# A three-slot Perceiver pipeline on one core: the block diagonals of head attention placed by SyncE, the first attention weights transposed on VectorE, the output bias added on GpSimd

## The chip, the cores and the metric

The kernel runs on one core of one Trainium2 chip. The metric is the device time of one execution in microseconds (us); the kernel before took 1451.5 us (median of three runs, 1449.05 to 1451.91).

The core has engines with instruction queues of their own: PE (TensorE) multiplies matrices and also transposes through an identity matrix, DVE (VectorE) and ACT (ScalarE) work element by element and read PE's results from PSUM, POOL (GpSimd) works on SBUF only, and SP (SyncE) only issues DMA transfers. Each engine runs its queue strictly in order. A semaphore wait at the head of a queue holds everything behind it.

## The reference, cut to what matters

There are 128 batch entries of 32 rows by 512 numbers. Each is normalized and goes through three blocks, each added to its input:

```python
x = x + xattn(layernorm(x), ctx)      # causal self attention, attention over 257 context rows, relu layer, norms
x = x + attn(layernorm(x))            # 16 heads of 32 columns, causal softmax times a decay, projection
x = x + ffn(layernorm(x))             # silu(x1) * x2, layer norm, second product, bias b3; experts for some rows

# the part of attn that the change touches
q, k, v = split(x @ W_attn)           # each cut into 16 heads
att = softmax(mask(q @ k.T / sqrt(32)))
att = att * decay
y = att @ v                           # per entry and head
# the part of xattn that it touches
p = softmax(mask(Q @ K.T) / sqrt(512))   # 32 x 32 per entry
a = p @ V + inputs
# the last step of the shared ffn
out = x2 + (z @ sw3.T + sb3)
```

Rows named by an index go a second time through one of eight experts; this is done at the end, and for the last tile inside the pipeline.

## The kernel before

Four entries of 32 rows stand together in one tile of 128 rows, so there are 32 tiles (0 to 31). A tile passes through all steps in four rounds. In each round four tiles are in work: the one just entered (lag 0), and those entered one, two and three rounds before (lags 1, 2, 3). Buffers exist three times (`rows1[s]`, `rows2[s]`, `rows3[s]`, `ps_a[s]`, `ps_t[s]` and others, with s the tile's number modulo 3; the third slot's SBUF buffers are parts of `last_slot`, which is the name that rows show for them).

The order on each engine is written out by hand. `FIRST` holds it for rounds 0 to 3, `ORDER` for rounds 4 to 29, `LAST` from round 30 on; `LOADS` holds it for SP in all rounds. An entry is a pair of a lag and a step's name, and `run_pipeline` issues the step for tile (round - lag). The same step name stands in the tables of several engines, each with its own part.

The steps around the change:

- `project_k`: PE computes the keys transposed, `high_t` and `low_t` (L1739, L1751), into `ps_a`. They must then stand in `kbd`, a block diagonal (for each entry and each group of four heads a 128 x 128 block in which each head's 32 keys fill their own 32 partitions), because `head_scores` on PE (L1814) handles four heads in one product. ACT writes the quarters of heads 0 and 1 (L850), DVE those of heads 2 and 3 (L1309).
- `head_scores`, `head_total`, `head_weights` on DVE: mask, maximum, subtraction, sum, reciprocal, product; then four 32-partition transposes (L1349) write the weights into `pbd`, a block diagonal over the four entries, for `head_mix` on PE (L1826). GpSimd multiplies by the decay (L653).
- `self_scores` on DVE scales, masks and takes the maximum; ACT exponentiates (L821); `turn_p` on PE transposes the 128 x 128 weights (L1770), ACT copies them to SBUF (L826), and `self_mix` on PE multiplies (L1775).
- `project_out` on DVE (L1355) makes x2 in `rows3`; `store_x2` on SP (L496) writes it to memory.
- `ffn_out` on DVE: one instruction for the product and b3 (L1389), one that adds x2 (L1391). `store` on SP (L500) writes the result.
- `xn_moments` and `turn_xn`: mean and variance of the tile just entered (L1178 to L1180), the inverse deviation on GpSimd (L636), the normalized rows on DVE (L1184), and their transposes on PE (L1703).

SP's order before, in a round: the next x, the context in transposed form (`load_ctx_t`, 2 MB, waits for the previous tile's `context_scores`), `store_x2` of the tile at lag 3, `store` of the same, then the context in plain form (`load_ctx_n`, 2 MB) and its last row (`ctx_last`).

## Time and profile before

| | |
|---|---|
| timed runs | 1451.91, 1449.05, 1451.5 us |
| profiled execution | span 1452.8 us; the page gives no time of its own beside the span, which lies 1.3 us above the median of the runs |
| busy | PE 1365.6 us (94%), weight loads 851.7, DVE 1128.1 (78%), ACT 601.9 (41%), POOL 526.1 (36%) |
| chain that ended last | PE 70%, DVE 19%, POOL 4%, ACT 4%, issue 3%, DMA 0% |
| DMA | 201.41 MB, 139 GB/s on the mean, busy three to four tenths |
| TensorE clock | nine tenths or more in 38 of the 40 slices, 8 tenths in the 2nd and the 38th |

A span is the time from the first to the last instruction. "PEclk" in a row of stretches is the clock that TensorE was granted, 1.00 for 2.4 GHz and 0.50 for 1.2 GHz. In a row of the time line the first number is the start, the second the duration, and what stands in brackets is the idle time before it and what ended it; nothing in brackets means that the engine was kept busy or that no releaser was found.

### The profile page before, as it was taken

The page shows a single profiled execution, that of the slowest core. Times are in us where ns is not written, and L with a number is a line of the kernel's source. Part 1 is how long each engine was busy: PE and PEld are TensorE (multiplying, and loading weights), DVE is VectorE, ACT ScalarE, POOL GpSimd, SP SyncE. Part 2 cuts the span into 40 slices and gives each one's busy share as a digit, 9 for nine tenths or more (in the row PEclk, how much of TensorE's full clock was granted, in tenths as well). Part 3 has the DMA queues.
Part 4 walks back from the last instruction along what each step waited for, and adds up shares of the span by engine and source line. Part 5 has one row for each costly group of instructions (what it writes and reads, how often), then busy time and mean ns, then how long its engine had stood idle before and what let it go on. Part 6 is the DMA issues. An engine that isn't in the chain of part 4 may idle for free.

```text
span 1452.8 us, 33270 instructions
## 1 busy us (share of the span) xinstructions
PE 1365.6 (94%) x13860; PEld 851.7 (59%) x13861; DVE 1128.1 (78%) x2335; ACT 601.9 (41%) x1147; POOL 526.1 (36%) x545
## 2 busy tenths in 40 slices
PE   7679999999999999999999999999999999998888
PEld 3355566666656666665665656666665666655443
DVE  6787777777787877778778877777778877777776
ACT  2544444443444444343434444444444444443222
POOL 0133333433444333443443333343443433343222
PEclk9899999999999999999999999999999999999899
DMA  9732444433333444433333344443333344434440
GB/s 349 259 131 74 146 146 146 144 123 105 133 112 115 146 146 146 146 137 101 122 130 105 139 146 146 146 142 114 111 138 105 123 146 146 147 134 161 149 161 30
DMA packets 38662, 201.41 MB, mean 139 GB/s; under 512 B 5096, under 2 KB 5992, under 8 KB 28400
## 3 DMA queue, kind: packets, MB, share of 16 engines
q1 hardware_dynamic: 37648, 198.93, 38.3%
q8 instruction: 109, 1.79, 0.5%
q10 hardware_dynamic: 864, 0.36, 0.1%
q14 instruction: 41, 0.34, 0.1%
HBM read 182.24 MB, written 17.04 MB: 137 GB/s over the span
## 4 chain that ended last, share of the span: by engine, by line
PE 70%; DVE 19%; POOL 4%; ACT 4%; issue 3%; DMA 0%; DVEq 0%; POOLq 0%; ACTq 0%; SPq 0%
PE ps_a L1716 11%; PE ps_a L1739 8%; PE ps_t L1739 7%; PE ps_t L1703 6%; PE ps_a L1725 6%; PE ps_a L1751 4%; PE ps_a L1783 4%; POOL rstd L636 4%; PE ps_t L1716 3%; PE ps_v L1716 3%; DVE stats L1178 3%; DVE arena L1309 3%; PE ps_t L1826 2%; PE ps_t L1775 2%; PE ps_t L1751 2%
## 5 line engine op out<-in xcount | busy, mean ns | idle before, releaser
L645 POOL TENSOR_TENSOR act_l<-act_t,act_h 128x512 f16<-128x512 f32 (+1 forms) x176 | 199.5, 1134 | 351.4 <-ACT act_t L789 199.4
L636 POOL TENSOR_TENSOR rstd<-var,mhalf 128x1 f32<-128x1 f32 x224 | 181.8, 812 | 333.7 <-DVE var L1180 328.9
L781 ACT ACTIVATE act_h<-ps_t,scale 128x512 f16<-128x512 f32 (+1 forms) x110 | 70.8, 644 | 206.2 <-PE ps_t L1703 206.2
L645 POOL TENSOR_TENSOR last_slot<-last_slot 128x512 f16<-128x512 f32 x80 | 90.0, 1125 | 156.7 <-ACT last_slot L789 90.8
L1739 PE MATMUL ps_a<-act_h,arena 128*128 128x128 f16 x1408 | 87.6, 221 | 17.3 <-ACT act_h L781 17.3
L1739 PEld LDWEIGHTS ps_a<-act_h,arena 128*128 128x128 f16 x1408 | 81.9, 99 | 28.3 <-ACT act_h L781 21.3
L789 ACT ACTIVATE act_t<-ps_t,scale 128x512 f32<-128x512 f32 (+1 forms) x110 | 70.3, 639 | 49.1 <-PE ps_t L1703 49.1
L1739 PE MATMUL ps_t<-act_h,arena 128*128 128x128 f16 x1408 | 87.0, 221 | 3.3 <-ACT act_h L781 3.3
L1716 PE MATMUL ps_a<-arena,act_h 128*128 128x512 f16 x352 | 83.6, 380 | 1.9 <-ACT act_h L781 1.9
L1309 DVE TENSOR_SCALAR arena<-ps_a,unscale 32x512 f32<-32x512 f32 x64 | 48.2, 753 | 47.0 <-PE ps_a L1751 45.8
L1739 PEld LDWEIGHTS ps_t<-act_h,arena 128*128 128x128 f16 x1408 | 81.4, 99 | 4.9 <-DVE arena L1037 2.4
L1178 DVE BATCH_NORM_STATS2 stats<-rows 128x6 f32<-128x512 f32 x110 | 76.5, 695 | 3.8
L781 ACT ACTIVATE last_slot<-ps_t,scale 128x512 f16<-128x512 f32 (+1 forms) x50 | 32.2, 644 | 89.4 <-PE ps_t L1703 89.4
L1191 DVE SCALAR_TENSOR_TENSOR rows<-rows,rstd,beta 128x512 f32<-128x512 f32 x66 | 50.2, 761 | 22.3 <-POOL rstd L636 22.2
L1716 PE MATMUL ps_a<-w_parts,act_h 128*128 128x512 f16 x264 | 64.2, 379 | 2.0 <-ACT act_h L781 2.0
L1703 PE MATMUL ps_t<-ident,rows 128*128 128x128 f32 x352 | 56.1, 283 | 9.1 <-DVE rows L1184 7.4
L1349 DVE STREAM_TRANSPOSE arena<-rows 32x512 f32<-32x512 f32 x88 | 61.8, 703 | 2.8
L1799 PE MATMUL ps_a<-arena,p_t 128*32 128x512 f32 x512 | 62.6, 607 | 0.0
L1716 PEld LDWEIGHTS ps_a<-arena,act_h 128*128 128x128 f16 x352 | 31.3, 98 | 50.6 <-ACT act_h L781 10.5
L1703 PEld LDWEIGHTS ps_t<-ident,rows 128*128 128x128 f32 x352 | 41.0, 143 | 29.0 <-DVE rows L1184 20.1
L1187 DVE SCALAR_TENSOR_TENSOR rows<-rows,mv,gamma 128x512 f32<-128x512 f32 x66 | 50.3, 762 | 0.0
L1783 PE MATMUL ps_a<-arena,q_t 128*32 128x257 f32 x704 | 44.2, 393 | 4.7 <-ACT q_t L830 4.7
(380 smaller groups left out, 3150.7 us busy)
## 6 DMA issues: line engine op xcount, KB each, us to landing
arena<-in_ctx_t SPq DMA_DIRECT2D x32, 2056.0 KB, 8.4
arena<-in_ctx_n SPq DMA_DIRECT2D x32, 2048.0 KB
ctx_last<-in_ctx_last SPq DMA_DIRECT2D x32, 256.0 KB
arena<-in_ew SPq DMA_DIRECT2D x8, 1024.0 KB, 6.3
x_in<-in_x SPq DMA_DIRECT2D x22, 256.0 KB, 7.3
x_scratch<-rows SPq DMA_DIRECT2D x22, 256.0 KB, 8.8
out<-rows SPq DMA_DIRECT2D x22, 256.0 KB, 2.1
arena<-in_ew SPq DMA_DIRECT2D x8, 512.0 KB, 7.2
```

The costliest lines, as they stand in the source:

```text
L636: nc.gpsimd.tensor_tensor(rstd[s][:], var[s][:], mhalf[:], ALU.pow).then_inc(rstd_ready[s], 1)
L645: nc.gpsimd.tensor_tensor(act_l[s][:, chunks], act_t[s][:, chunks], act_h[s][:, chunks], ALU.subtract).then_inc(act_l_ready[s], 1)
L781: nc.scalar.activation(act_h[s][:, 0:width // P].rearrange("p c r -> p (c r)"), bank[s][:, 0:width], ACT.Copy, scale=scale[:, k:k + 1]).th ...
L789: nc.scalar.activation(act_t[s][:, 0:width // P].rearrange("p c r -> p (c r)"), bank[s][:, 0:width], ACT.Copy, scale=scale[:, k:k + 1]).th ...
L1178: chain(nc.vector.bn_stats(stats[s][:], rows))
L1309: nc.vector.tensor_scalar(kbd[rows, :, :, h, :], ps_a[s][rows, :].rearrange("p (c g k) -> p c g k", c=C, g=G), unscale[rows, K_WATTN:K_WAT ...
L1703: mm = nc.tensor.transpose(out[s][:, c * P:(c + 1) * P], rows[s][:, lo + c * P:lo + (c + 1) * P], ident[:])
L1716: nc.tensor.matmul(bank[s][:], act_h[s][:, c, :], w[:, part, c, lo:lo + D], start=(c == 0 and part == 0), stop=False, skip_group_check=True)
L1725: mm = nc.tensor.matmul(bank[s][:], act_l[s][:, c, :], w[:, 0, c, lo:lo + D], start=False, stop=(c == chunks - 1), skip_group_check=True)
L1739: nc.tensor.matmul(bank[s][:, m * P:(m + 1) * P], w[:, part, c, lo + m * P:lo + (m + 1) * P], act_h[s][:, c, :], start=(m == 0 and c == 0 ...
L1751: mm = nc.tensor.matmul(bank[s][:, m * P:(m + 1) * P], w[:, 0, c, lo + m * P:lo + (m + 1) * P], act_l[s][:, c, :], start=False, stop=(c == ...
L1783: mm = nc.tensor.matmul(ps_a[s][T * g:T * (g + 1), 0:S], q_t[s][:, c, T * g:T * (g + 1)], ctx_t[:, c, g, :], start=(c == 0), stop=(c == C ...
```

## The change

- `project_k`: ACT writes all keys in one instruction, dense, into `rows3` of the slot (semaphore `k_out`). DVE's two instructions are gone. A new step `heads_k` on SP copies them by four SBUF to SBUF transfers of 64 KB (one for each 32 partitions) into `kbd`; PE's `head_scores` waits for all four. `kbd` is laid out anew, with the head outermost, so that a partition's 2 KB are contiguous at the destination; PE now reads 4 pieces of 32 numbers each.
- `head_weights`: DVE transposes once over 128 partitions into `rows3` (`heads_turned`), and a new step `heads_p` on SP copies to `pbd` by four transfers of 64 KB; `head_mix` waits for them.
- `turn_p` moves from PE and ACT to DVE, as one 128 x 128 instruction that transposes 32 x 32 blocks, together with the reciprocal that `self_mix` had.
- `ffn_out` is one DVE instruction. b3 is added ahead of it to x2 in `rows3` by the new step `x2_bias` on GpSimd, which waits until x2 is normalized and until `store_x2` has landed.
- The scale of the exponent goes into `unscale`, so that the negative maximum comes straight from the reduction: one small instruction less in `self_scores` and `context_scores`.
- Some waits of DVE for its own previous instruction move from behind it to the instruction that reads the result (`made_by`).

```diff
-LOADS = [(0, "load_x"), (0, "set_first"), (0, "set_rest"), (0, "load_ctx_t"),
+LOADS = [(0, "load_x"), (0, "set_first"), (0, "set_rest"), (0, "load_ctx_t"), (2, "heads_k"),
          (3, "store_x2"), (1, "e_first"), (1, "e_second"), (1, "e_rows"), (2, "e_fifth"), (3, "store"),
-         (0, "load_ctx_n"), (1, "e_third"), (1, "e_fourth"), (2, "e_sixth")]
+         (0, "load_ctx_n"), (2, "heads_p"), (1, "e_third"), (1, "e_fourth"), (2, "e_sixth")]
...
+                def heads_k(s, r, tile):
+                    sp.wait_ge(k_out, tile + 1)
...
+                    for h in range(HPC):
+                        mine = slice(HD * h, HD * (h + 1))
+                        sp.dma_start(kbd[mine, h, :, :, :].rearrange("p c g k -> p (c g k)"), rows3[s][mine, :]
+                                     ).then_inc(k_ready, 16)
+
+                def heads_p(s, r, tile):
+                    sp.wait_ge(heads_turned, tile + 1)
...
+                    for g in range(G):
+                        mine = slice(T * g, T * (g + 1))
+                        sp.dma_start(pbd[mine, g, :, :].rearrange("p h q -> p (h q)"), rows3[s][mine, :]
+                                     ).then_inc(pbd_ready, 16)
...
+                def x2_bias(s, r, tile):
+                    pool.wait_ge(rows_ready[s], 6 * r + 5)
+                    pool.wait_ge(x2_stored[s], 16 * r + 32)
...
+                    nc.gpsimd.tensor_tensor(rows3[s][:], rows3[s][:], b3[:], ALU.add).then_inc(x2_biased, 1)
...
                 def project_k(s, r, tile):
                     act.wait_ge(k_done[s], r + 1)
...
-                    for h in (0, 1):
-                        rows = slice(HD * h, HD * (h + 1))
-                        nc.scalar.activation(kbd[rows, :, :, h, :],
...
+                    nc.scalar.activation(rows3[s][:], ps_a[s][:], ACT.Copy, scale=unscale[:, K_WATTN:K_WATTN + 1]
+                                         ).then_inc(k_out, 1)
...
+                def turn_p(s, r, tile):
+                    chain = Chain("turn_p", s, r)
+                    dve.wait_ge(p_ready[s], 3 * r + 1)
+                    nc.vector.transpose(p_t[s][:, 0:P], p_n[s][:, 0:P]).then_inc(p_t_ready[s], 1)
+                    chain.last(nc.vector.reciprocal(inv[s][:, 0:1], total[s][:, 0:1]))
...
-                    for g in range(G):
-                        rows = slice(T * g, T * (g + 1))
-                        nc.vector.transpose(pbd[rows, :, g, :], by_head(rows1[s][rows, :])).then_inc(pbd_ready[s], 1)
+                    nc.vector.transpose(sc, by_head(rows1[s][:])).then_inc(heads_turned, 1)
...
                 def ffn_out(s, r, tile):
                     dve.wait_ge(rows_done[s], 6 * r + 6)
-                    chain = Chain("ffn_out", s, r)
-                    chain(nc.vector.scalar_tensor_tensor(rows2[s][:], ps_a[s][:], unscale[:, K_W3:K_W3 + 1], b3[:],
-                                                         ALU.mult, ALU.add))
-                    nc.vector.tensor_tensor(rows2[s][:], rows2[s][:], rows3[s][:], ALU.add).then_inc(out_ready[s], 1)
-                    chain.end()
+                    dve.wait_ge(x2_biased, tile + 1)
+                    nc.vector.scalar_tensor_tensor(rows2[s][:], ps_a[s][:], unscale[:, K_W3:K_W3 + 1], rows3[s][:],
+                                                   ALU.mult, ALU.add).then_inc(out_ready[s], 1)
...
-                pe.wait_ge(pbd_ready[s], 4 * r + 4)
+                pe.wait_ge(pbd_ready, 64 * (tile + 1))
```

The tables of DVE lose `project_k` and gain `turn_p` between `context_norm` (lag 1) and `self_mix` (lag 0); those of PE and ACT lose `turn_p`; those of POOL gain `x2_bias` (lag 3) ahead of `xn_moments` (lag 0).

Three places show what this does to the queues. First SP in a regular round, before. `arena` is the buffer that holds weights, context and the block diagonals.

```order
L482 DMA arena<-in_ctx_t 128x4112 [waits scored1]
L496 DMA x_scratch<-last_slot 128x512 [waits x2_ready2]
L500 DMA out<-last_slot 128x512 [waits out_ready2]
L489 DMA arena<-in_ctx_n 128x4096 [waits v_done1]
L492 DMA ctx_last<-in_ctx_last 128x1x512 [waits v_ready1]
L475 DMA x_in<-in_x 128x512 [waits x_used0]
L482 DMA arena<-in_ctx_t 128x4112 [waits scored2]
```

The same round of SP with the change (L510 is `heads_k`, L521 is `heads_p`):

```order
L482 DMA arena<-in_ctx_t 128x4112 [waits scored1]
L510 DMA arena<-rows 32x512 [waits scored2,k_out]
L510 DMA arena<-rows 32x512 x3
L496 DMA x_scratch<-last_slot 128x512 [waits x2_ready2]
L500 DMA out<-last_slot 128x512 [waits out_ready2]
L489 DMA arena<-in_ctx_n 128x4096 [waits v_done1]
L492 DMA ctx_last<-in_ctx_last 128x1x512 [waits v_ready1]
L521 DMA arena<-rows 32x512 [waits y_done2,heads_turned]
L521 DMA arena<-rows 32x512 x3
L475 DMA x_in<-in_x 128x512 [waits x_used0]
```

The store of x2 (L496), which stood right behind the context load, now stands behind a wait for the keys of the tile at lag 2 and four issues.

Second, DVE between `z_norm` of the tile at lag 3 and the normalized rows of the tile at lag 0, before:

```order
L1191 SCALAR_TENSOR_TENSOR last_slot<-last_slot,rstd,ln_b 128x256 [waits rstd_ready2,dve_step2]
L1309 TENSOR_SCALAR arena<-ps_a,unscale 32x16x32 [waits scored2,k_done0]
L1309 TENSOR_SCALAR arena<-ps_a,unscale 32x16x32
L1389 SCALAR_TENSOR_TENSOR last_slot<-ps_a,unscale,b 128x512 [waits rows_done2]
L1391 TENSOR_TENSOR last_slot<-last_slot 128x512 [waits dve_step2]
L1178 BN_STATS stats<-last_slot 128x6 [waits x_loaded2]
L1179 BN_AGGR mv<-stats 128x2 [waits dve_step2]
L1180 TENSOR_SCALAR var<-mv 128x1 [waits dve_step2]
L1246 RECIPROCAL inv<-total 128x1 [waits p_ready1]
L1184 TENSOR_SCALAR last_slot<-last_slot,mv,rstd 128x512 [waits rstd_ready2]
```

DVE there with the change:

```order
L1218 SCALAR_TENSOR_TENSOR last_slot<-last_slot,rstd,ln_b 128x256 [waits dve_step2,rstd_ready2]
L1399 SCALAR_TENSOR_TENSOR last_slot<-ps_a,unscale,last_slot 128x512 [waits x2_biased,rows_done2]
L1204 BN_STATS stats<-last_slot 128x6 [waits x_loaded2]
L1205 BN_AGGR mv<-stats 128x2 [waits dve_step2]
L1206 TENSOR_SCALAR var<-mv 128x1 [waits dve_step2]
L1273 RECIPROCAL inv<-total 128x1 [waits p_ready1]
L1210 TENSOR_SCALAR last_slot<-last_slot,mv,rstd 128x512 [waits rstd_ready2]
```

Three instructions are gone; the one that makes the output (L1399) now waits for GpSimd, and what the tile at lag 0 needs stands behind it.

Third, DVE between the self scores of the tile at lag 0 and its mix, before (L1268 to L1187 is `context_out` of the tile at lag 1, L1227 is `self_mix`):

```order
L1213 SCALAR_TENSOR_TENSOR last_slot<-ps_a,unscale,mask_self 128x128 [waits x2_stored2,scored2]
L1216 TENSOR_REDUCE top<-last_slot 128x1 [waits dve_step2]
L1217 TENSOR_SCALAR ntop<-top 128x1 [waits dve_step2]
L1268 SCALAR_TENSOR_TENSOR rows<-ps_a,row_out,rows 128x512 [waits rows_done1]
L1178 BN_STATS stats<-rows 128x6 [waits dve_step1]
L1179 BN_AGGR mv<-stats 128x2 [waits dve_step1]
L1180 TENSOR_SCALAR var<-mv 128x1 [waits dve_step1]
L1187 SCALAR_TENSOR_TENSOR rows<-rows,mv,gamma 128x512
L1191 SCALAR_TENSOR_TENSOR rows<-rows,rstd,beta 128x512 [waits rstd_ready1,dve_step1]
L1224 RECIPROCAL inv<-total 128x1 [waits p_ready2]
L1227 SCALAR_TENSOR_TENSOR last_slot<-ps_t,inv,last_slot 128x512 [waits out_stored2,rows_done2,dve_step2]
```

With the change (L1296 to L1213 is `context_out`, L1249 the new transpose, L1258 `self_mix`):

```order
L1240 SCALAR_TENSOR_TENSOR last_slot<-ps_a,unscale,mask_self 128x128 [waits x2_stored2,scored2]
L1243 TENSOR_REDUCE ntop<-last_slot 128x1 [waits dve_step2]
L1296 SCALAR_TENSOR_TENSOR rows<-ps_a,row_out,rows 128x512 [waits dve_step1,rows_done1]
L1204 BN_STATS stats<-rows 128x6 [waits dve_step1]
L1205 BN_AGGR mv<-stats 128x2 [waits dve_step1]
L1206 TENSOR_SCALAR var<-mv 128x1 [waits dve_step1]
L1213 SCALAR_TENSOR_TENSOR rows<-rows,mv,gamma 128x512
L1218 SCALAR_TENSOR_TENSOR rows<-rows,rstd,beta 128x512 [waits dve_step1,rstd_ready1]
L1249 STREAM_TRANSPOSE p_t<-p_n 128x128 [waits p_ready2]
L1250 RECIPROCAL inv<-total 128x1
L1258 SCALAR_TENSOR_TENSOR last_slot<-ps_t,inv,last_slot 128x512 [waits out_stored2,dve_step2,rows_done2]
```

Before, PE transposed these weights as soon as ACT had them; now the transpose stands behind five instructions for the tile at lag 1 and GpSimd's inverse deviation.

## Rows read from the trace of the kernel before

**Rows 1.** Busy times of a stretch: length, busy us of each engine, PEclk, DMA share, GB/s.
```profile
400.00:1200.00 800.00, 777.21 (x8357) 494.95 (x8355) 633.82 (x1322) 342.58 (x670) 315.96 (x315) 1.00 0.37 130
```

**Rows 2.** Time line of SP's issues, round 15 and the start of round 30.
```profile
634.72 0.33 SPq L482 DMA_DIRECT2D arena<-in_ctx_t  x1
635.09 0.43 SPq L496 DMA_DIRECT2D x_scratch<-rows  x1
644.82 0.34 SPq L500 DMA_DIRECT2D out<-rows  x1
646.20 0.34 SPq L489 DMA_DIRECT2D arena<-in_ctx_n  x1
...
1244.22 0.33 SPq L482 DMA_DIRECT2D arena<-in_ctx_t  x1
```

**Rows 3.** The chain that ended last, in order of time, in round 15.
```profile
640.82 0.91 PE ps_a L1751 x16
641.75 0.75 DVE arena L1309
...
643.32 0.76 DVE rows L1389
644.10 0.69 DVE rows L1391
...
647.07 0.66 PE ps_t L1703 x4
```

**Rows 4.** Time line of ACT, round 15.
```profile
642.03 1.37 ACT L850 ACTIVATE arena<-ps_a,unscale 32x512 f32<-32x512 f32 x2
...
644.32 0.69 ACT L856 ACTIVATE q_t<-ps_t,unscale 128x512 f32<-128x512 f32 x1 [0.52 <-PE ps_t L1751]
```

**Rows 5.** DMA issues: KB each, median us from issue to landing.
```profile
out<-rows SPq DMA_DIRECT2D x22, 256.0 KB, 2.1
```

**Rows 6.** Groups of instructions, 400 to 1200 us: busy, mean ns, idle before.
```profile
L653 POOL TENSOR_TENSOR rows<-rows,decay 128x512 f32<-128x512 f32 x13 | 16.6, 1280 | 12.4 <-ACT rows L866 12.4
```

**Rows 7.** Time line of PE, round 15.
```profile
645.95 1.06 PE L1814 MATMUL ps_a<-arena,q_t 128*32 128x128 f32 x32
...
659.16 0.27 PE L1770 MATMUL ps_a<-ident,p_n 128*128 128x128 f32 x1
...
660.38 1.13 PE L1775 MATMUL ps_t<-v_n,p_t 128*128 128x512 f32 x2
```

**Rows 8.** Time line of DVE, round 15.
```profile
654.13 2.90 DVE L1349 STREAM_TRANSPOSE arena<-rows 32x512 f32<-32x512 f32 x4
...
657.84 0.74 DVE L1268 SCALAR_TENSOR_TENSOR last_slot<-ps_a,row_out,last_slot 128x512 f32<-128x512 f32 x1
...
660.88 0.75 DVE L1191 SCALAR_TENSOR_TENSOR last_slot<-last_slot,rstd,beta 128x512 f32<-128x512 f32 x1 [0.51 <-POOL rstd L636]
```

**Rows 9.** Busy times of two stretches in round 2, columns as in rows 1.
```profile
101.00:104.00 3.00, 1.04 (x12) 0.72 (x9) 2.40 (x2) 1.11 (x2) 0.55 (x1) 0.93 0.67 170
104.00:107.00 3.00, 3.00 (x31) 3.00 (x30) 2.86 (x8) 0.73 (x3) 2.70 (x2) 0.50 0.99 422
```

**Rows 10.** The chain that ended last, round 2: one product's two halves.
```profile
103.72 3.48 PE ps_a L1739 x32
107.20 1.79 PE ps_t L1739 x32
```

**Rows 11.** Time line of SP's issues, round 32.
```profile
1331.95 0.47 SPq L518 DMA_DIRECT2D last_slot<-x_scratch  x1
...
1344.06 0.33 SPq L545 DMA_DIRECT2D ctx_last<-in_sel_g  x1
```

**Rows 12.** Time line of DVE, round 32.
```profile
1338.78 1.54 DVE L1309 TENSOR_SCALAR arena<-ps_a,unscale 32x512 f32<-32x512 f32 x2 [1.43 <-PE ps_a L1751]
...
1346.41 0.69 DVE L1404 BATCH_NORM_STATS2 stats<-last_slot 128x6 f32<-128x512 f32 x1 [1.02 <-DMA last_slot<-x_scratch]
...
1360.96 0.69 DVE L1480 TENSOR_TENSOR last_slot<-ps_a,arena 128x512 f32<-128x512 f32 x1
```

More of the change, by code:

```diff
@@ L146 @@
         (1, "e_gate_c"), (1, "e_bias0"), (2, "e_bias3"), (0, "self_scores"), (2, "e_z3"), (1, "e_z0"),
-        (1, "context_out"), (0, "self_mix")],
+        (1, "context_out"), (0, "turn_p"), (0, "self_mix")],
     "act": [(3, "head_mix_t"), (3, "head_mix"), (2, "turn_h2"), (2, "turn_h2_t"), (2, "e_zt0"), (2, "e_gate1"),
@@ L820, in self_scores @@
                     act.wait_ge(ntop_ready[s], 2 * r + 1)
-                    nc.scalar.activation(p_n[s][:, 0:P], rows3[s][:, 0:P], ACT.Exp, bias=ntop[s][:], scale=XSCALE,
+                    nc.scalar.activation(p_n[s][:, 0:P], rows3[s][:, 0:P], ACT.Exp, bias=ntop[s][:],
                                          accum_out=total[s][:, 0:1]).then_inc(p_ready[s], 1)
-                def turn_p(s, r, tile):
-                    act.wait_ge(p_turned[s], 2 * r + 1)
-                    nc.scalar.copy(p_t[s][:, 0:P], ps_a[s][:, 0:P]).then_inc(p_t_ready[s], 1)
                 def project_query(s, r, tile):
@@ L843, in project_k @@
                     act.wait_ge(k_done[s], r + 1)
-                    if tile == 0:
-                        act.wait_ge(consts_ready, 4)
-                    else:
-                        act.wait_ge(scored[(s - 1) % SLOTN], 3 * (r - (s == 0)) + 3)
-                    for h in (0, 1):
-                        rows = slice(HD * h, HD * (h + 1))
-                        nc.scalar.activation(kbd[rows, :, :, h, :],
-                                             ps_a[s][rows, :].rearrange("p (c g k) -> p c g k", c=C, g=G), ACT.Copy,
-                                             scale=unscale[rows, K_WATTN:K_WATTN + 1]).then_inc(k_ready[s], 1)
+                    nc.scalar.activation(rows3[s][:], ps_a[s][:], ACT.Copy, scale=unscale[:, K_WATTN:K_WATTN + 1]
+                                         ).then_inc(k_out, 1)
                 def project_q(s, r, tile):
@@ L1167, in __call__, with last @@
                     def __call__(self, ins):
+                        self.last(ins)
+                        dve.wait_ge(dve_step[self.s], steps_in_all * self.r + steps_before[self.unit] + self.count)
+                    def last(self, ins):
                         self.count += 1
@@ L1270, in context_out @@
                     moments(chain, s, rows3[s][:], 1e-3)
-                    chain(scaled(s, rows1[s][:], rows3[s][:], gamma[:]))
+                    chain.last(scaled(s, rows1[s][:], rows3[s][:], gamma[:]))
                     chain.end()
                 def context_norm(s, r, tile):
-                    offset(s, r, 3, rows1[s][:], beta[:]).then_inc(rows_ready[s], 1)
+                    offset(s, r, 3, rows1[s][:], beta[:], "context_out").then_inc(rows_ready[s], 1)
                 def hidden(s, r, tile):
@@ L1285, in hidden @@
                     moments(chain, s, rows3[s][:], 1e-3)
-                    chain(scaled(s, rows2[s][:], rows3[s][:], gamma[:]))
+                    chain.last(scaled(s, rows2[s][:], rows3[s][:], gamma[:]))
                     chain.end()
@@ L1369, in ffn_in @@
                     chain = Chain("ffn_in", s, r)
-                    chain(nc.vector.scalar_tensor_tensor(v_n[s][:, H:], rows2[s][:, 0:H], 0.5, rows2[s][:, H:],
+                    chain.last(nc.vector.scalar_tensor_tensor(v_n[s][:, H:], rows2[s][:, 0:H], 0.5, rows2[s][:, H:],
                                                          ALU.mult, ALU.mult))
@@ L1766, in self_scores @@
                     mm.then_inc(scored[s], 1)
-                def turn_p(s, r, tile):
-                    pe.wait_ge(p_ready[s], 3 * r + 1)
-                    nc.tensor.transpose(ps_a[s][:, 0:P], p_n[s][:, 0:P], ident[:]).then_inc(p_turned[s], 1)
                 def self_mix(s, r, tile):
@@ L1810, in head_scores @@
                     pe.wait_ge(q_ready[s], 4 * r + 4)
-                    pe.wait_ge(k_ready[s], 4 * r + 4)
+                    pe.wait_ge(k_ready, 64 * (tile + 1))
                     for c in range(C):
```

131 lines of the change are left out of this document (63 added, 68 removed), and 1 row of the table FIRST.

## The prediction

> **What bounds the kernel now.** I read the busy times by stretch first. In 800 us of regular rounds PE is busy 777.2 us, DVE 633.8, at the full clock throughout [rows 1]: PE is the bound, and all that it ever idles there is 22.8 us, 1.16 us in a round. A round is the distance between two context loads: from 634.72 (round 15) to 1244.22 (round 30) 609.5 us, so 40.63 us [rows 2]. Nothing that unloads DVE, ACT or PE's waits can give back more than that 1.16 us. Then I read the chain of waits in order of time, because PE's slack is thin in one place: after the keys of the tile at lag 2 (end 641.73) the chain leaves PE, runs through DVE (block diagonal, output, moments) and GpSimd, and comes back at 647.07 with the transposes of the tile just entered [rows 3]. PE has other work meanwhile, and that work ends just when DVE delivers. Whatever makes DVE later between 641.7 and 647.1 is paid one for one. Last I read SP's time line, since the change puts waits into that queue.
>
> **Part 1: the output waits for GpSimd, GpSimd for the store, the store for the keys.** Taken away on DVE are the two block diagonal writes (1.54 us) and the addition L1391 (0.69) [rows 3, 12]. In their place stands a wait. I follow it through round 15. PE ends the keys at 641.73. ACT starts on them at 642.03, behind its exponentials, and one full instruction takes 0.69 us [rows 4]: keys in SBUF at 642.72. SP issues four transfers. One issue behind another started 0.37 us apart (634.72 to 635.09), and the second took 0.43 itself [rows 2]; I take 0.45 each, 1.8 us. Only then comes the store of x2, which went out at 635.09 before: now at about 644.6. A 256 KB store into an idle queue lands 2.1 us after its issue [rows 5]: 646.7. GpSimd adds b3; the nearest row is its 128x512 product with the decay, 1.28 us [rows 6]: 648.0. DVE starts the output there and not at 643.32, that is 4.8 us later [rows 3]; since L1391 (0.78 from start to start) is gone, the moments of the new tile start 4.0 us later. GpSimd's inverse deviation and the normalization follow as before, so PE's transposes start at about 651.1. PE idles for the **4.0 us**. Bounds: issues at 0.37 and the landing at 2.0 make it 3.6; issues at 0.55 and 1.4 us more for a store that mixes with the 256 KB of the four transfers make it 5.8.
>
> What is queued behind this wait on DVE is all of the rest of the round, but its later instructions follow the same tile or PE itself, so they shift with PE and add nothing. In the same gap hides the latency of the block diagonal of the keys: its transfers land at about 646.5, PE's `head_scores` needs them at 645.95 [rows 7], and PE would idle until 651.1 anyway. If that cover were gone it would cost some 0.6 us.
>
> The Trainium skill (DMA: Bandwidth & Descriptors, Anatomy of one DMA) gives a fixed part of about 2.0 us and 436 GB/s on top, fitted for transfers issued by GpSimd: 2.6 us for this store, where the row has 2.1. With the page's price the sum would be 14 us higher; the row decides.
>
> **Part 2: the head weights.** DVE's four transposes (2.90 us, 0.73 each) become one, and four transfers follow [rows 8]. In the new time scale DVE ends that transpose about 7.8 us after PE's transposes start (654.13 less 647.07, plus 0.7), SP issues until 9.6, the last lands at about 11.7 by the 2.1 us of [rows 5]. PE needs the block at 12.1 after (659.16 less 647.07) [rows 7]. It fits with 0.4 us to spare, provided the plain context load, which SP issued at 646.20 [rows 2] and which will now go out about 3.5 us later behind the delayed store of the output, is through. Cost nothing; without that cover 1 to 3 us a round. PE reads its block in four pieces now; the trace has no such operand. Below: nothing gained; above: the 1.08 us product could double. I take nothing.
>
> **Part 3: the transpose of the self weights on DVE.** PE loses L1770, whose successor starts 0.20 us later; the product behind it ran until 660.38 [rows 7]. But DVE puts the transpose behind `context_out` and `context_norm` of the other tile. Freed from the block transposes, DVE can start L1268 at about 656.8, when PE has its product, instead of 657.84 [rows 8]. From there to the end of L1191 the trace has 3.79 us (657.84 to 661.63), with GpSimd's deviation inside: 660.6. The transpose: one of 512 columns takes 0.73, so one of 128 between 0.2 and 0.4; with 0.3: 660.9. PE would be ready for `self_mix` at 660.2; before it started at 660.38. So it starts **0.5 us** later than before, and the removed work is already in this number. Bounds 0.2 (a faster transpose) and 0.9 (the same chain with a later start).
>
> **Part 4: the clock of TensorE.** In round 2, PE was busy 1.04 us in the 3 us from 101 to 104, and in the next 3 us the granted clock was 0.50, the lower of its two levels, 1.2 GHz [rows 9]. The first half of a product of 64 small matmuls then took 3.48 us, the second half, at the full clock, 1.79 [rows 10]: 1.7 us lost. With the change PE has in every round a stretch like it: about 0.6 us idle ahead of `head_scores`, that product, and some 3.4 us idle behind it. I expect the clock to fall in most rounds, sometimes before the gap's end so that part of the low time costs nothing: **1.3 us** a round on the mean; bounds 0 and 2.3.
>
> The Trainium skill (TensorE: Matmul & The Clock Gate, HAM oscillation) tells that a kernel whose matmuls wait for a transfer in every iteration pays the half clock in every iteration. The trace agrees in the one place where it has such a gap; regular rounds of before have none.
>
> **Part 5: the ends.** In rounds 0 to 3 DVE is itself on the path and gains a little, the store chain costs once (round 3): +4 us together. The end costs more. In round 32 SP used to read x2 of the last routed tile back at 1331.95, behind ten expert issues, because nothing held it; it is awaited by DVE at 1346.41 [rows 11, 12]. Now all this stands behind the keys of tile 30, which PE has at 1338.78 [rows 12]: 0.75 us for ACT, 1.8 for the block, 0.45 for the store, 4.7 for the ten issues at the 0.47 of [rows 11]: read back at 1346.5, and by the same 14.4 us as before landed at 1360.9: 14.5 late. The expert biases were issued at 1344.06 [rows 11]; now they stand behind the head weights, which DVE had done some 0.9 us before it added the first bias at 1360.96 [rows 12], and will have at 1360.1 - 2.2 + 14.5 = 1372.4. With 1.8 for the block, 4.6 for their own eight issues and about 5.5 to land (an estimate, above the 2.1 of rows 5 because 2 MB stand in the queue): 1384.3, so 23.3 late in all. Round 33 adds the store chain (4.0) and the weights' transfers on an exposed chain (3.9 for 2.2): 5.7; the dropped addition gives 0.7 back. Together **+28 us**; bounds 12 (the read-back lands sooner, since only part of the 5 MB is ahead) and 38.
>
> **The sum.** 28 regular rounds (4 to 31) at 4.0 + 0.5 + 1.3 = 5.8 us: 162. With 4 and 28: 194. The profiled execution spans 1452.8 us, 1.3 above the median of the runs: 1452.8 + 194 - 1.3 = **1646 us**. Lowest terms: 3.6 + 0.2 + 0 for 28 rounds, 0, 12: 1570. Highest: 5.8 + 1.1 + 0.9 + 2.3 for 28 rounds, 10, 38: 1782.
>
> **Rivals.**
> A, the clock holds: everything else as above, 28 x 1.3 less: 1610. For it: gaps of about 1 us in regular rounds left the clock at 1.00 [rows 1]. Against: [rows 9]. 25%.
> B, the head weights' transfers queue behind the plain context load and its last row, which now starts later; PE waits again at `head_mix`, 2.5 us a round: 1646 + 70 = 1716. For it: the 0.4 us of spare time is thin. Against: GpSimd and DVE leave the queue 10 us from the load's issue. 12%.
> C, the other side: the bias is added in time and DVE's relief decides. It holds only if x2's store lands and GpSimd is done before DVE reaches the output, at 641.8 instead of 648.0; then PE loses L1770 (0.2 us a round) and some of its 1.16 us: about 1451.5 - 28 x 0.3 = 1443. For it: DVE does lose about 4.4 us of work a round. Against: the order of SP's queue leaves the store no way past the keys. 3%; no change at all 2%.
> The forecast itself: 58%.
>
> **Chances.** Slower by over 0.2% (about what a measurement of this kernel can tell from no change) 0.95, within 0.2% 0.02, faster 0.03. The range for 8 in 10, across the forecast and most of A and B: 1590 to 1708.
>
> **What would show it.** Right: SP's store of x2 issued 10 us after the context load, not 0.4; DVE idle some 7 us before the output instruction with GpSimd's addition as its releaser; PE idle about 3.4 us before L1703's counterpart with DVE as releaser; a second idle of 0.5 us before `self_mix`; a round of 46 to 47 us; PEclk below 1.00 in regular rounds; DVE's first expert moments 15 us late against PE's keys in round 32. Wrong: a round under 43 us, or a store that is issued before the keys' transfers.

## The result, and the profile after

The changed kernel takes **1713.69 us** (median of four runs, 1712.18 to 1714.39) where the kernel before, on the same chip, takes 1451.7 (1449.05 to 1452.14): ratio 1.181, interval 1.180 to 1.183. The forecast was 1646 us with a range of 1590 to 1708. The direction and the mechanism came as predicted; the time lies 68 us above the forecast and 6 us outside the range. The question is therefore which terms were too small.

Busy times of the stretch from 400 to 1200 us of the changed kernel, columns as in [rows 1]:

```profile
400.00:1200.00 800.00, 691.59 (x7092) 428.18 (x7092) 464.40 (x1002) 278.44 (x539) 286.68 (x283) 0.94 0.36 124
```

PE is idle 108.4 us of these 800 where it was idle 22.8, and the granted clock is 0.94 instead of 1.00. DVE works 169 us less in the same time: some 74 of that are relief (4.4 us a round, an estimate from these busy times and the lengths of a round), the rest comes from fewer rounds in the 800 us. More waiting and a slower clock, with no engine busier than before: no engine has become the bound, a chain has. A round, from context load to context load, has 47.8 us (732.91 to 780.78) instead of 40.63.

SP's issues in the round that begins at 732.91 (start, duration), to be laid beside [rows 2]:

```profile
732.91 0.33 SPq L482 DMA_DIRECT2D arena<-in_ctx_t  x1
740.95 2.41 SPq L510 DMA_DIRECT2D arena<-rows  x4
743.40 0.58 SPq L496 DMA_DIRECT2D x_scratch<-rows  x1
747.94 0.35 SPq L500 DMA_DIRECT2D out<-rows  x1
...
759.94 2.44 SPq L521 DMA_DIRECT2D arena<-rows  x4
```

The store of x2 goes out 10.5 us behind the context load and no longer 0.37. The four issues ahead of it take 2.41 us, 0.61 each from start to start. The same chain on ACT, POOL and DVE, from the keys' way into SBUF to the normalized rows of the new tile:

```profile
740.22 0.70 ACT L869 ACTIVATE rows<-ps_a,unscale 128x512 f32<-128x512 f32 x1
...
745.80 1.26 POOL L685 TENSOR_TENSOR rows<-rows,b 128x512 f32<-128x512 f32 x1 [5.10 <-DMA x_scratch<-rows]
...
747.16 0.75 DVE L1399 SCALAR_TENSOR_TENSOR rows<-ps_a,unscale,rows 128x512 f32<-128x512 f32 x1 [8.79 <-POOL rows L685]
...
749.59 0.55 DVE L1210 TENSOR_SCALAR rows<-x_in,mv,rstd 128x512 f32<-128x512 f32 x1 [0.59 <-POOL rstd L658]
```

Each releaser is the one of the prediction: DVE's output waits for POOL, POOL for the store. PE in the same round:

```profile
738.84 1.06 PE L1759 MATMUL ps_a<-act_l,arena 128*128 128x128 f16 x16
...
744.90 1.08 PE L1818 MATMUL ps_a<-arena,q_t 128*32 128x128 f32 x32 [0.57 <-DMA arena<-rows]
750.19 1.12 PE L1711 MATMUL ps_t<-ident,rows 128*128 128x128 f32 x4 [4.21 <-DVE rows L1210]
751.10 3.43 PE L1724 MATMUL ps_v<-arena,act_h 128*128 128x512 f16 x8
...
764.33 1.08 PE L1830 MATMUL ps_t<-arena,v_n 128*32 128x128 f32 x32
765.86 1.12 PE L1779 MATMUL ps_t<-v_n,p_t 128*128 128x512 f32 x2 [0.45 <-DVE p_t L1249]
```

The first row is that of the keys, done at 739.90 (738.84 and 1.06). Then four things are to be seen: `head_scores` waits a little for the keys' transfers, the transposes wait 4.21 us for DVE, the product behind them takes 3.43 us (1.89 elsewhere), and `self_mix` waits 0.45 us for DVE's transpose. `head_mix` (L1830) waits for nothing here. The clock of the gap and of the product, in stretches of 1 us (length, busy times, then PEclk, third from the end):

```profile
745.00:746.00 1.00, 0.98 (x32) 0.71 (x31) 0.00 (x0) 0.00 (x0) 0.20 (x1) 1.00 0.19 72
746.00:747.00 1.00, 0.00 (x0) 0.00 (x0) 0.00 (x0) 0.00 (x0) 1.00 (x1) 1.00 0.00 0
747.00:748.00 1.00, 0.00 (x0) 0.00 (x0) 0.84 (x2) 0.00 (x0) 0.06 (x1) 0.69 0.00 0
...
753.00:754.00 1.00, 1.00 (x4) 0.30 (x2) 0.32 (x2) 1.00 (x3) 0.84 (x1) 0.50 0.96 410
754.00:755.00 1.00, 1.00 (x14) 0.79 (x13) 0.95 (x3) 0.73 (x2) 0.81 (x1) 0.90 1.09 459
```

The clock falls to its lower level, 1.2 GHz, while PE idles, and stays there through the product. From the transposes (750.19) to the next projection (754.36) the trace has 4.17 us. Before, at the full clock, the same stretch took 2.22, from 647.07 [rows 3] to this row:

```profile
649.29 1.95 PE L1739 MATMUL ps_a<-act_h,arena 128*128 128x128 f16 x32
```

So 1.95 us are lost. The Trainium skill (TensorE: Matmul & The Clock Gate, HAM oscillation) describes a kernel whose products wait for a transfer in every iteration and start every iteration at the half clock. The trace agrees, with a wait for DVE in place of the transfer: the granted clock is 0.94 from 400 to 1200 us, where it was 1.00.

### The profile page after: what moved, and what is told of

It reads as the page before. It is cut to its first block and busy times, and to the rows that moved or that the text cites. A ratio compares the mean times of both kernels' runs of the same rounds, so it can differ in the third digit from the quotient of the medians.

```text
span 1710.4 us, 33273 instructions
## 1 busy us (share of the span) xinstructions
PE 1427.2 (83%) x13828; PEld 866.9 (51%) x13829; DVE 989.3 (58%) x2112; ACT 575.1 (34%) x1083; POOL 564.7 (33%) x577
## 5 line engine op out<-in xcount | busy, mean ns | idle before, releaser
L1711 PE MATMUL ps_t<-ident,rows 128*128 128x128 f32 x352 | 64.0, 312 | 98.8 <-DVE rows L1210 95.0
L1399 DVE SCALAR_TENSOR_TENSOR rows<-ps_a,unscale,rows 128x512 f32<-128x512 f32 x22 | 16.5, 751 | 192.7 <-POOL rows L685 192.7
L1711 PEld LDWEIGHTS ps_t<-ident,rows 128*128 128x128 f32 x352 | 45.5, 156 | 119.5 <-DVE rows L1210 106.8
L1711 PE MATMUL ps_t<-ident,last_slot 128*128 128x128 f32 x220 | 37.4, 292 | 41.5 <-DVE last_slot L1210 41.1
L1724 PE MATMUL ps_v<-arena,act_h 128*128 128x512 f16 x176 | 70.0, 571 | 0.0
L685 POOL TENSOR_TENSOR rows<-rows,b 128x512 f32<-128x512 f32 x22 | 27.8, 1262 | 115.3 <-DMA x_scratch<-rows 107.0
L1399 DVE SCALAR_TENSOR_TENSOR last_slot<-ps_a,unscale,last_slot 128x512 f32<-128x512 f32 x10 | 7.5, 751 | 91.5 <-POOL last_slot L685 91.5
```

The source lines that it names most:

```text
L685: nc.gpsimd.tensor_tensor(rows3[s][:], rows3[s][:], b3[:], ALU.add).then_inc(x2_biased, 1)
L1399: nc.vector.scalar_tensor_tensor(rows2[s][:], ps_a[s][:], unscale[:, K_W3:K_W3 + 1], rows3[s][:], ALU.mult, ALU.add).then_inc(out_ready[s], 1)
L1711: mm = nc.tensor.transpose(out[s][:, c * P:(c + 1) * P], rows[s][:, lo + c * P:lo + (c + 1) * P], ident[:])
L1724: nc.tensor.matmul(bank[s][:], act_h[s][:, c, :], w[:, part, c, lo:lo + D], start=(c == 0 and part == 0), stop=False, skip_group_check=True)
```

## The experiments

The theory (T) is the chain of the prediction, with the sizes of the trace after: keys, four issues, store, addition, output, transposes, and the clock that falls in the gap. All runs are whole kernels; each edit is made to the changed kernel, except in `before_bias`.

**Moving the store ahead of the keys** (store_first):

```diff
-LOADS = [(0, "load_x"), (0, "set_first"), (0, "set_rest"), (0, "load_ctx_t"), (2, "heads_k"),
-         (3, "store_x2"), (1, "e_first"), (1, "e_second"), (1, "e_rows"), (2, "e_fifth"), (3, "store"),
+LOADS = [(0, "load_x"), (0, "set_first"), (0, "set_rest"), (0, "load_ctx_t"), (3, "store_x2"),
+         (2, "heads_k"), (1, "e_first"), (1, "e_second"), (1, "e_rows"), (2, "e_fifth"), (3, "store"),
```

> SP issues the store of x2 before it waits for the keys, all else as in the changed kernel. Theory T (the store stands behind the keys' wait and four issues, GpSimd's addition behind its landing, DVE's output and all of lag 0 behind that, and the clock falls in the gap): the wait of DVE L1399 for GpSimd goes, the clock stays at 1.00, and what is left of a round's loss is PE's wait for the keys' own transfers (0.9 us) and the late self_mix (0.4): a round of 41.9 us, 1520 us in all (1500 to 1545, the end still about 30 late). Rival U (the loss lies in the eight transfers themselves, or in PE's reading of the new block layouts): above 1650 us.

Measured: 1551.03 us (1549.35 to 1553.94), ratio 1.070 (1.068 to 1.071). The 163 us that go show that the place of one issue in SP's queue carries most of the loss, and rule U out. The 31 us above my figure are a miss, outside T's range. The mean round has 42.7 us, not 41.9, which makes 20 of them; the rest is mostly the opening (context load 4 at 199.50, before at 188.32). SP's, POOL's and DVE's rows of the round that begins at 757.26:

```profile
757.64 0.43 SPq L496 DMA_DIRECT2D x_scratch<-last_slot  x1
...
766.73 1.29 POOL L685 TENSOR_TENSOR last_slot<-last_slot,b 128x512 f32<-128x512 f32 x1 [1.68 <-DMA x_scratch<-last_slot]
...
768.12 0.75 DVE L1399 SCALAR_TENSOR_TENSOR last_slot<-ps_a,unscale,last_slot 128x512 f32<-128x512 f32 x1 [5.40 <-POOL last_slot L685]
```

The store was issued at once and landed 9 us later, beside 2 MB of context that was issued 0.38 us ahead of it. DVE still waits 5.4 us, PE 0.78 (and 0.60 for the keys); the usual round has 42.5 us, some 45 to 47. The transfer of 2.1 us in [rows 5] was one into an idle queue. That the store of x2 is slow in this place stood in the trace of before (KB, median us from issue to landing), where nobody waited for it, and T could have priced it:

```profile
x_scratch<-rows SPq DMA_DIRECT2D x22, 256.0 KB, 8.8
```

The Trainium skill (DMA: Bandwidth & Descriptors, Issuing engines are not separate DMA queues) says that DMAs run on the same 16 engines and interleave, whoever issues them. The 8.8 us of the median store here fit that, beside a load with a median of 8.6. Whether the store is served between the load's pieces or behind them, no run shows.

**Undoing the addition on GpSimd** (bias_undone; `x2_bias` also leaves GpSimd's tables):

```diff
-                    dve.wait_ge(x2_biased, tile + 1)
-                    nc.vector.scalar_tensor_tensor(rows2[s][:], ps_a[s][:], unscale[:, K_W3:K_W3 + 1], rows3[s][:],
-                                                   ALU.mult, ALU.add).then_inc(out_ready[s], 1)
+                    chain = Chain("ffn_out", s, r)
+                    chain(nc.vector.scalar_tensor_tensor(rows2[s][:], ps_a[s][:], unscale[:, K_W3:K_W3 + 1], b3[:],
+                                                         ALU.mult, ALU.add))
+                    nc.vector.tensor_tensor(rows2[s][:], rows2[s][:], rows3[s][:], ALU.add).then_inc(out_ready[s], 1)
+                    chain.end()
...
```

> DVE makes the output in two instructions again with b3 and x2, GpSimd's addition is gone, SP's order stays as changed, with the store of x2 behind the keys. Theory T: cutting the chain at this link does the same as moving the store: 1525 us, within 10 us of it; the 0.69 us more on DVE hides. Rival V (it is the late store, and behind it the late store of the output and the late plain context load, that hold the round, not the addition): above 1600 us.

Measured: 1531.14 us (1528.32 to 1533.95), round 41.65. V is out: SP's late store hurts by the addition that waits for it, not by itself. The round is 1.02 us above before, and PE's rows name it: 0.59 for the keys' transfers (the 0.6 that the prediction gave them without their cover), 0.45 for DVE's transpose. Of the 74 us that this trace is longer than that of before, 12 lie ahead of round 4, 31 in rounds 4 to 30 and 31 behind the last context load.

**Store between the wait and the issues** (store_between): `heads_k` waits for the keys, then issues the store of x2, then its four transfers.

> The store of x2 still stands behind SP's wait for the keys, but ahead of the four issues. Theory T with the size read from the trace of the changed kernel (four issues of 0.61 us each, where I had taken 0.45): the store goes 2.45 us earlier and 26 rounds get 2.4 us shorter, 1645 us (1630 to 1665). With issues of 0.45 us it would be 1663. Rival W (the size error came from the store's landing beside the four transfers, which now start together with it): the gain is under 1 us a round, above 1688 us.

Measured: 1603.55 us (1594.96 to 1608.15), 41 us better than T's figure and outside its range. The store is no slower beside the transfers (DVE's output starts 3.6 us after its issue, 3.8 in the changed kernel), so W is out. Rounds come in two lengths, 43.3 and 45.0 us: 47.8 less 2.45 is 45.35, and less the 1.95 of the clock 43.4. The transposes of two rounds and the product behind them show it:

```profile
749.82 1.11 PE L1717 MATMUL ps_t<-ident,rows 128*128 128x128 f32 x4 [1.19 <-DVE rows L1216]
750.73 3.08 PE L1730 MATMUL ps_v<-arena,last_slot 128*128 128x512 f16 x8
...
794.69 0.66 PE L1717 MATMUL ps_t<-ident,last_slot 128*128 128x128 f32 x4 [1.12 <-DVE last_slot L1216]
795.18 1.89 PE L1730 MATMUL ps_v<-arena,act_h 128*128 128x512 f16 x8
```

The wait for DVE is down from 4.21 us to 1.2 (the keys' transfers, issued behind the store, now hold `head_scores` longer), and the clock falls in some rounds only. T forgot that the gain of a shorter wait can come twice.

**Keeping the clock up in the gap** (clock_kept):

```diff
                     mm.then_inc(scored[s], 1)
+                    if 3 <= tile <= 27:
+                        for n in range(16):
+                            nc.tensor.matmul(ps_e[:], w3[:, 0, 0, 0:P], w3[:, 0, 0, :], start=True, stop=True,
+                                             skip_group_check=True)
```

> As the changed kernel, but PE does 16 extra half-precision products of 512 columns into a bank that nobody reads, behind head_scores of tiles 3 to 27 (some 3.5 us at the full clock), in the gap where it waits for the transposes of lag 0. The chain of the store is untouched. Theory T: the clock stays at 1.00, the self projection takes its full speed again, 1.95 us a round in 25 rounds: 1665 us (1655 to 1685). Rival X (the clock cost nothing, what looks slow was waiting for something else): 1705 to 1720 us.

Measured: 1667.86 us (1667.37 to 1670.13), 45.8 us less than the changed kernel by work that nobody needs. Its round has 45.93 us, 1.9 less than 47.83, and PE's rows show the gap filled and the product at its full speed:

```profile
727.36 3.63 PE L1825 MATMUL ps_e<-w_parts 128*128 128x512 f16 x16
731.63 0.66 PE L1711 MATMUL ps_t<-ident,rows 128*128 128x128 f32 x4 [0.64 <-DVE rows L1210]
732.13 1.89 PE L1724 MATMUL ps_v<-arena,act_h 128*128 128x512 f16 x8
```

The clock term is shown, with its size: 1.9 us a round.

**The store ahead of the context load** (bias_early_store): `(3, "store_x2")` stands before `(0, "load_ctx_t")`.

> SP issues the store of x2 ahead of the context load and not behind it (in the run with the store merely ahead of the keys it landed 9 us after its issue, beside 2 MB of context, and GpSimd's addition still came 5.4 us late for DVE). Theory T (only the landing of the store makes the addition late): the store lands in some 2.3 us, long before the keys are done, DVE waits for GpSimd no more, and the round is that of the run with the addition undone, 41.65 us: 1530 us (1520 to 1540). Rival Y (the addition itself holds GpSimd's queue in a bad place, or slows DVE): above 1540 us.

Measured: 1526.42 us (1525.73 to 1529.8), usual round 41.65. The median store lands 2.1 us after its issue, and PE waits for nothing of the chain any more. So the addition on GpSimd is free once its store is early; the 187 us between this run and the changed kernel are the price of its place, not of its work. Y is out.

**The transpose of the self weights earlier** (turn_p_early): in DVE's tables for rounds 0 to 29 `(0, "turn_p")` stands before `(1, "context_norm")`.

> As the changed kernel, with DVE's transpose of the self weights ahead of context_norm of the other tile, where DVE waits 0.44 us for GpSimd anyway, in rounds 0 to 29. Theory T: PE's 0.45 us ahead of self_mix goes (1.76 us in rounds 1 to 3), and every round gets shorter by that: 1713.7 less 26 x 0.43 less 4 is 1698 us (1690 to 1704). Rival: the wait only moves to the next thing that DVE makes (x2 or the norm for the other tile): 1709 to 1718 us.

Measured: 1707.2 us (1701.98 to 1708.23), ratio 1.175 against 1.181: 6.5 us, not 16, between the ranges of T and of the rival. PE's wait of 0.45 is gone, but the round only fell from 47.83 to 47.76. The rest went into the clock. Its stretches at the start and the end of the low time, in the round from 919.32 (PE idle from 932.4, transposes at 936.63):

```profile
933.00:934.00 1.00, 0.00 (x0) 0.00 (x0) 0.39 (x1) 0.00 (x0) 0.51 (x1) 1.00 0.00 0
934.00:935.00 1.00, 0.00 (x0) 0.00 (x0) 0.96 (x3) 0.00 (x0) 0.00 (x0) 0.79 0.00 0
...
940.00:941.00 1.00, 1.00 (x4) 0.35 (x3) 0.86 (x4) 1.00 (x3) 0.65 (x2) 0.50 0.94 393
941.00:942.00 1.00, 1.00 (x16) 1.00 (x15) 0.53 (x2) 0.18 (x1) 0.91 (x1) 0.79 0.77 311
```

The transposes start earlier in the low time here than in the changed kernel: the clock is back some 4.8 us after their start, there some 4.0. The product takes 3.62 us instead of 3.43 and the projection behind it 2.17 instead of 1.95, together 0.4 us. In all of six rounds between 746 and 986 us that product has 3.62. What a wait saved, the low clock took. That both are one effect is read from the rows; no run varied this alone.

**The head weights written by DVE** (weights_direct): four transposes into `pbd`, no transfers.

> As the changed kernel, but DVE writes the head weights into their block diagonal itself, by four transposes of 32 partitions, and the four transfers are gone. Theory T: in regular rounds the transfers cost PE nothing, but they relieve DVE of 2.2 us on the way to the transpose of the self weights, so undoing them makes self_mix about 1.0 us later: +26 us; in rounds 2 and 3, where head_mix stands early and PE waited 2.6 and 1.9 us for the transfers, it gives 4.5 back: 1735 us (1722 to 1745). Rival Z (the transfers cost the round something through the queues): at or under 1713 us.

Measured: 1727.02 us (1725.84 to 1727.86). Undoing this part alone makes the kernel slower by 13 us. PE's wait before `self_mix` grew from 0.45 to 1.32 us, as reckoned, since DVE has 2.2 us more ahead of its transpose. The 13 us are a balance: rounds 4 to 29 take 31 us more, the parts outside them less. In round 2 the load of the next context came 4.2 us sooner (44.14 against 48.35 us for the round), in round 3 1.4, and from the last context load to the end it has 198.0 us against 209.1: there the transfers do cost. At the end DVE no longer waits for the expert biases, which stood behind them in SP's queue (12.9 us in the changed kernel).

**The expert loads ahead of the keys** (experts_first), on top of store_first:

```diff
-         (2, "heads_k"), (1, "e_first"), (1, "e_second"), (1, "e_rows"), (2, "e_fifth"), (3, "store"),
-         (0, "load_ctx_n"), (2, "heads_p"), (1, "e_third"), (1, "e_fourth"), (2, "e_sixth")]
+         (1, "e_first"), (1, "e_second"), (1, "e_rows"), (2, "heads_k"), (2, "e_fifth"), (3, "store"),
+         (0, "load_ctx_n"), (1, "e_third"), (2, "heads_p"), (1, "e_fourth"), (2, "e_sixth")]
```

> As the run with the store of x2 ahead of the keys (1551 us), and the expert loads and the read-back of x2 also ahead of the keys, the expert biases ahead of the head weights. It concerns round 32 alone. Theory T (the end's loss, 30.4 us there after the last context load, is mostly these loads standing behind keys and head weights): it falls by 20 to 25 us, 1529 us (1524 to 1536). Rival (the end loses by the transfers of keys and weights in an exposed chain, and the loads hardly matter): above 1543 us.

Measured: 1531.01 us (1527.68 to 1537.4), 20 less than store_first. From the last context load to the end it has 176.1 us, store_first 197.1, before 166.7. DVE's wait for the read-back of x2 fell from 17.19 us to 1.88:

```profile
1424.28 0.70 DVE L1412 BATCH_NORM_STATS2 stats<-last_slot 128x6 f32<-128x512 f32 x1 [1.88 <-DMA last_slot<-x_scratch]
```

**The keys written by ACT and DVE** (keys_direct): `project_k` on both engines as before, no transfers, SP's order else as changed.

> As the changed kernel, but ACT and DVE write the keys' block diagonal and the four transfers are gone, SP's order otherwise the same: the store of x2 follows the context load at once. Theory T: it lands 9 us after its issue, as in the run with the store ahead of the keys, the addition is as late as there, and PE loses about as much per round (42.3 to 42.6 us); the end is shorter, since only the last expert loads stand behind the head weights: 1535 us (1520 to 1550). Rival (without the transfers of the keys the addition is in time): under 1505 us.

Measured: 1536.24 us (1528.68 to 1543.19), in T's range, with a mean round of 43.0 us (a little above T's) and most of them 41.5 to 43.1. The store follows the context load at once and is as late as in store_first. Without the early store, taking the keys off SP does not save the addition.

**What is left of the change without transfers** (all_direct): keys and weights written directly, store ahead of the context load, `turn_p` early.

> The changed kernel without its eight transfers (ACT and DVE write the keys' block diagonal, DVE that of the weights), with the store of x2 ahead of the context load and DVE's transpose of the self weights ahead of context_norm. What stays of the change: the addition of b3 on GpSimd, the self weights' transpose on DVE, the negated maximum, the own waits at their consumers. Theory T: PE is the bound; of its 1.11 us of waits in a round of before (0.78 for ACT behind the transposes of x1, 0.33 for DVE behind those of x2) none is touched, so DVE's relief gives nothing, and PE saves the transpose alone, 0.20 us a round: 40.43 us a round, 1446 us, ratio 0.996 (0.993 to 0.999). Rival: DVE's relief of some 1.5 us a round also shortens PE's waits, below 1440 us; or an addition on GpSimd costs DVE, above 1452 us.

Measured: 1449.97 us (1444.78 to 1450.83, 11 runs) against 1449.63, ratio 0.9995 (0.9986 to 1.0004): no change. The round has 40.54 us, 0.10 less than before and not 0.20. DVE works 11.8 us less in the stretch of 800 (622.01, before 633.82), and it gains nothing to see. Neither T's range nor the rival's holds the result. 26 rounds at 0.10 would give 2.6 us, and the median lacks them. Ten of the eleven executions have a mean granted clock of 0.987 or 0.988; the eleventh has 0.992 and took 1444.78. Of the sixteen executions of before, fourteen have 0.991 or 0.992. So the clock outside the regular rounds may take back what they give; no run varied that alone.

**The kernel before with the early addition alone** (before_bias): the added step, the one-instruction output and `(3, "store_x2")` ahead of `(0, "load_ctx_t")`.

> The kernel before with one part of the change: b3 is added on GpSimd and DVE makes the output in one instruction; SP issues the store of x2 ahead of the context load so that the addition is in time. Theory T: DVE loses 0.69 us a round that nobody waited for, PE's two waits stay, 1450 us, ratio 1.000 (0.998 to 1.002). Rival: DVE was on the path between the keys and the new tile's transposes, and PE's round gets shorter by some of it: ratio under 0.996.

Measured: 1445.7 us (1444.94 to 1447.84), ratio **0.9966** (0.9953 to 0.9978). It is faster than before by 3.9 us, little but clear of the interval, and neither side's figure was quite right. The round is 40.50 us, 0.13 less. The place is the one the prediction called thin: `head_scores` to the transposes of the new tile, 1.12 us apart in [rows 3, 7] (645.95, 647.07) and now 0.99, the time that the product itself needs:

```profile
806.77 1.06 PE L1819 MATMUL ps_a<-arena,last_slot 128*32 128x128 f32 x32
807.76 0.66 PE L1708 MATMUL ps_t<-ident,rows 128*128 128x128 f32 x4
```

Before, DVE delivered 0.13 us late, too little for the trace to show as a wait; the 0.69 of the dropped addition removed that and no more. This is read from the rows: no run moved the store without dropping the addition. 26 rounds at 0.13 are 3.4 us of the 3.9 between the medians. The two traces also differ behind the last context load (163.1 against 166.7 us), but they are single executions, and from 1350 to 1360 us the granted clock is 0.85 here and 0.52 in that of before.

## Why the time was missed: the prediction's steps, one by one

The mechanism of every large term held, and four sizes failed: the chain of the store (4.0 us a round forecast, 4.9 measured, most of it the issues at 0.45 us each that take 0.61), the clock (1.3 forecast, 1.95 measured), the opening (4 forecast, 18.3 measured, with the exposed head weights of rounds 2 and 3 not priced at all) and the end.

**The output waits for GpSimd, GpSimd for the store, the store for the keys** (Part 1): right in every link, too small in size. Predicted from the end of the keys to DVE's output 6.27 us, measured 7.26 (739.90 to 747.16). Of the 0.99 us, 0.65 are the issues: a 64 KB transfer from 32 partitions takes SP 0.61 us, and I had taken 0.45 from a load and a store of another shape. 0.3 are the store's landing (2.4 us to GpSimd's start, 2.1 assumed). ACT took the keys 0.3 us after their end, as forecast. PE's transposes start 10.29 us after the end of the keys, before 5.34: 4.9 us later, not 4.0. The 4.0 also holds a slip: 648.0 less 643.32 is 4.7 and not 4.8, so the sum should have had 3.9. The upper bound of 5.8 held it. store_between, bias_undone and bias_early_store show the chain link by link.

**The head weights** (Part 2): right for regular rounds, where PE waits for nothing at `head_mix`, and where the transfers even help DVE (weights_direct). Wrong for rounds 2 and 3, which I had not worked out: their table has `head_mix` earlier on PE, ahead of `self_scores`, so that the transfers are exposed (2.58 and 1.87 us). The table stood in the code. The operand in pieces, for which I took nothing, costs nothing to see: `head_scores` takes 1.08 us (1.06 before) and `head_mix` 1.08 as before.

**The transpose on DVE** (Part 3): 0.5 predicted, 0.45 waited; from the transposes of the new tile to `self_mix` it is 0.4 more than before, the clock's 1.95 taken off. Right.

**The clock** (Part 4): the mechanism right, and the 1.3 us were 0.65 too little: I averaged over rounds in which the clock would stay; at a gap of 4.2 us it fell in all that I looked at. 1.95 measured by duration, 1.9 by clock_kept. Rival A (the clock holds) was worth 25% and is dead. Round 2 was also not "the one place" of before with a gap and a low clock: it had 0.67 from 60 to 70 us and 0.52 from 1350 to 1360.

**The ends** (Part 5): the opening was to cost 4 us and cost 18.3 (context load 4 at 206.64 instead of 188.32). 4.9 of it are round 2: the exposed weights' transfers, and 1.76 us before `self_mix`, whose transpose stands in that table behind a whole `project_out`. 13.8 are round 3, where the chain of the store meets a table in which PE has nothing else to do:

```profile
169.00 1.11 PE L1711 MATMUL ps_t<-ident,rows 128*128 128x128 f32 x4 [8.26 <-DVE rows L1210]
...
185.28 1.08 PE L1830 MATMUL ps_t<-arena,v_n 128*32 128x128 f32 x32 [1.87 <-DMA arena<-rows]
192.78 1.12 PE L1779 MATMUL ps_t<-v_n,p_t 128*128 128x512 f32 x2 [1.76 <-DVE p_t L1249]
```

"The store chain costs once (round 3)" was the right thought with the wrong price. At the end, the read-back and the biases are awaited where I said, each a little later still:

```profile
1586.45 0.69 DVE L1412 BATCH_NORM_STATS2 stats<-last_slot 128x6 f32<-128x512 f32 x1 [12.67 <-DMA last_slot<-x_scratch]
1611.33 0.69 DVE L1488 TENSOR_TENSOR last_slot<-ps_a,arena 128x512 f32<-128x512 f32 x1 [12.88 <-DMA arena<-in_ew]
```

From the last context load they come at 85.2 and 110.1 us, before at 60.3 and 74.9. Against the end of PE's keys the moments are 16.8 us late (24.4, before 7.6), where I had 14.5. From the last context load to the end the loss is 42.4 us, where 28 and one round of 5.8 make 33.8. experts_first shows that, of the 30 us that store_first loses there, 20 are the order of these loads; weights_direct shows that 11 of the 42 go with the head weights' transfers. The two overlap, since the biases stand behind those transfers.

**The sum of the miss.** Opening 14.3; rounds 4 to 29 took 187.6 us more, not 26 x 5.8 = 150.8: 36.8; round 30 9.3, not 5.8: 3.5; from there on 8.6; and the profiled execution (1710.4) lies 3.3 below the median where before lay 1.3 above: 4.6. Together 67.8 us, against 67.7 measured. More than half are 1.4 us a round, from prices that were each a little small and count 28 times: the issues (0.65), the store's landing (0.3) and the clock (0.65), less 0.2 that the rows do not name. A fifth is an opening that I priced by analogy instead of reading its table.

The range missed by 6 us. Its upper end came from rival B (1716 cut to 1708), a mechanism that did not occur; the sum of my own upper bounds, 1782, was written down and then not used.

**Rivals.** B (the weights' transfers wait behind the plain context load): none of it in regular rounds. C (DVE's relief decides): with the store early the addition is in time, but the changed kernel then takes 1526.4 us, since the transfers remain. That before_bias comes to 1445.7, near C's 1443, is luck: it is another kernel, with neither the transfers nor DVE's new transpose. C's reason is worth 0.13 us a round there, and 0.10 in all_direct, where PE loses its transpose as well, and not 0.3.

## What to carry to other kernels

Before a wait is put into a queue that only issues, list what stands behind it there and which engine needs that; here one early entry for the store was worth 187 us. Price an issue by its own shape and multiply by the rounds: 0.16 us too little, four times in 28 rounds, are 18 us. A gap on PE costs its length and, where the clock falls in it, slower work behind it (1.9 us a round here). So a shorter gap can gain more than its length (store_between), and a wait that is removed elsewhere in the round can be lost to the low clock again (turn_p_early).

## What the runs showed of the hardware that I had not expected

- SP needs 0.61 us for each SBUF to SBUF transfer of 64 KB out of 32 partitions (four in 2.41 to 2.44 us in the rounds shown), where a 2 MB load of context takes it 0.33.
- A 256 KB store issued 0.4 us behind a 2 MB load lands after 8.8 us (median; store_first, and the kernel before), ahead of it after 2.1 (bias_early_store).
- 16 useless products in a gap made the kernel 45.8 us faster.
- DVE transposes 128x128 in blocks of 32x32 in 0.30 us, 128x512 in 0.71, as long as a single one of the four 32x512 pieces that it replaced (0.70).
